# A step's whole turns counted ahead of the scans of the step before it, and one planned cost raised

## The reference

```python
x = x + 0.5 * ffn(layernorm(x))     # 8 experts, top 2 of them, and a shared one
x = x + attn(layernorm(x))
x = x + 0.5 * ffn(layernorm(x))
# attn, K = 32 heads, H = 8, M = 8 angles
phi = k_val[..., None] * theta                  # b, l, K, H, M
re_k, im_k = cos(phi), sin(phi)
cs = cumsum(concat([p_w, p_w * re_k, p_w * im_k]), axis=1)
state_re, state_im = num_re / den, num_im / den
out_re = sum(state_re * q_re + state_im * q_im, axis=-1)
out_im = sum(state_im * q_re - state_re * q_im, axis=-1)
# a gated projection of out_re and out_im, and W_out
```

## Time and profile before

| | |
|---|---|
| median of 3 runs | 1212.84 us (1212.49 to 1217.21) |
| profiled execution, its own time | 1213.98 us |
| span of the profile | 1212.6 us |
| PE, DVE, ACT, POOL busy | 1038.2, 729.8, 647.4, 483.2 us |
| TensorE clock granted, mean | 0.94 |

### The profile page before, as it was taken

How to read it: one execution, slowest core, us unless ns; L and a number is a source line. 1 busy time by engine, 2 the same in 40 slices (tenths; PEclk the granted TensorE clock), 3 DMA queues, 4 the chain that set the end, 5 groups by cost and what they waited for, 6 DMA issues and landing times.

```text
span 1212.6 us, 11351 instructions
## 1 busy us (share of the span) xinstructions
PE 1038.2 (86%) x3424; PEld 570.9 (47%) x3424; DVE 729.8 (60%) x1210; ACT 647.4 (53%) x1104; POOL 483.2 (40%) x451
## 2 busy tenths in 40 slices
PE   5887999868899889899879979985987899979993
PEld 3454544534445554334545434442554644436661
DVE  2320017698899899689969978994996931200000
ACT  4343334488546685445775675344588851414441
POOL 3454522353525542431632414521483431155542
PEclk9988999989999989899879989987999999989997
DMA  9876662666735866653856754353785763225666
GB/s 315 303 238 157 117 147 61 166 156 114 156 112 135 216 159 124 166 140 92 234 123 132 180 121 128 100 147 79 161 192 119 153 112 63 69 79 99 114 109 104
DMA packets 68978, 172.54 MB, mean 142 GB/s; under 512 B 12355, under 2 KB 12355, under 8 KB 66791
## 3 DMA queue, kind: packets, MB, share of 16 engines
q0 software_dynamic: 32576, 72.44, 33.2%
q1 hardware_dynamic: 36342, 99.38, 26.6%
HBM read 112.86 MB, written 68.33 MB: 149 GB/s over the span
## 4 chain that ended last, share of the span: by engine, by line
PE 31%; ACT 7%; DMA 5%; issue 3%; DVE 3%; POOL 1%; SPq 1%; DVEq 0%; ACTq 0%; POOLq 0%
PE hps L854 7%; PE yps L870 6%; PE misc L932 5%; PE yps L812 5%; PE hps L800 4%; DMA outT<-tail_sb 2%; DMA out_rows<-ys,into_i 1%; DMA x_rows<-ys,rows_i 1%; ACT L1036 1%; ACT ys L1049 1%; ACT hidden_sb L1036 1%; PE misc L923 1%; SPq L1855 1%; PE xps L923 1%; PE xps L845 1%
## 5 line engine op out<-in xcount | busy, mean ns | idle before, releaser
L870 PE MATMUL yps<-w_all,hidden_sb 128*128 x424 | 213.9, 629 | 39.7 <-ACT hidden_sb L1036 39.5
L854 PE MATMUL hps<-w_all,hidden_sb 128*128 x848 | 219.0, 404 | 25.3 <-ACT hidden_sb L1036 16.4
L1641 POOL DMA_INDIRECT xs<-x_normal,rows_i x106 | 124.1, 1171 | 216.2 <-PE xps L845 164.7
L854 PEld LDWEIGHTS hps<-w_all,hidden_sb 128*128 128x128 f32 x848 | 166.1, 202 | 80.7 <-issue 60.8
L1441 DVE TENSOR_TENSOR_SCAN run<-pwx,trig 128x512 f32<-128x512 f32 x128 | 149.3, 1207 | 24.8 <-ACT trig L1124 24.4
L1665 POOL DMA_INDIRECT x_rows<-ys,rows_i x56 | 101.6, 1813 | 105.5 <-ACT ys L1049 99.1
L870 PEld LDWEIGHTS yps<-w_all,hidden_sb 128*128 128x128 f32 x424 | 81.3, 200 | 117.8 <-issue 115.1
L1049 ACT ACTIVATE ys<-yps,slots 128x512 f32<-128x512 f32 x106 | 73.0, 689 | 110.9 <-PE yps L870 90.4
L800 PE MATMUL hps<-xnT,sw_sb 128*128 128x512 f32 x256 | 120.9, 621 | 6.5 <-ACT hidden_sb L1009 6.5
L812 PE MATMUL yps<-sw_sb,hidden_sb 128*128 128x512 f32 x256 | 120.8, 615 | 0.0
L1627 POOL DMA_INDIRECT slots<-told,dest_i x64 | 75.3, 1176 | 54.0 <-DVE cmp_a L1310 30.3
(11 more groups left out here) (202 smaller groups left out, 1531.1 us busy)
## 6 DMA issues: line engine op xcount, KB each, us to landing
qx<-q_cols SPq DMA_DIRECT2D x128, 256.0 KB
w_all<-in_w_experts SPq DMA_DIRECT2D x8, 1024.0 KB, 10.3
x_normal<-xin SPq DMA_DIRECT2D x32, 256.0 KB, 4.6
xin<-x_rows SPq DMA_DIRECT2D x32, 256.0 KB, 6.7
turns_sb<-in_w_out SPq DMA_DIRECT2D x3, 1536.0 KB, 13.7
xin<-in_x SPq DMA_DIRECT2D x16, 256.0 KB, 5.3
sum_rows<-ys SPq DMA_DIRECT2D x16, 256.0 KB, 3.0
xin<-sum_rows POOLq DMA_DIRECT2D x16, 256.0 KB, 8.2
```

Of the source, the lines that this page charges most:

```text
L854: t = PE.matmul(hps[:, bank, 0:H], xT[:, j % 2, c, :], w_all[:, bass.ds(expert[j] + c * H, H)], start=c == 0, stop=c == KC - 1)
L870: t = PE.matmul(yps[:, bank, :], hb[:, j % 2, ec, :], w_all[:, bass.ds(expert[j] + (KC * H + ec * D), D)], start=ec == 0, stop=ec == EC - 1)
L1641: GE.indirect_dma_start(xs[:, j % NX, :], None, xn_rows[PAIR_OF[g]], bass.IndirectOffsetOnAxis(rows_i[:, g % 2, j:j + 1], 0)).then_inc(*xs ...
```

## The change

Two edits. One raises the planned cost of the DVE stage `("load", 7)` from 1.2 to 11; the stage's instructions stay as they are. The other splits `phases`: the whole-turns instruction, with the waits that it had, becomes `whole_turns`, stage `c_int`. The DVE list is gone through after the planning: where a `c_scan` is directly followed by a `c_turn`, that turn's `c_int` is put in front of the scan; where a `c_turn` follows anything else, its `c_int` stands directly in front of it, as before.

```diff
-            piece("DVE", ("load", q), 1.2 if q == NJ - 1 else 3.4, ("SP", ("fetch", q), 3.6),
+            piece("DVE", ("load", q), 11 if q == NJ - 1 else 3.4, ("SP", ("fetch", q), 3.6),
...
         ORDERS = orders()
+        VECTOR = []
+        for i, s in enumerate(ORDERS["DVE"]):
+            then = ORDERS["DVE"][i + 1] if i + 1 < len(ORDERS["DVE"]) else ("end",)
+            if s[0] == "c_scan" and then[0] == "c_turn":
+                VECTOR.append(("c_int", *then[1:]))
+            if s[0] == "c_turn" and ORDERS["DVE"][i - 1][0] != "c_scan":
+                VECTOR.append(("c_int", *s[1:]))
+            VECTOR.append(s)
...
-            def phases(b, n):
+            def whole_turns(b, n):
                 half, m = divmod(n, M)
-                s = n % 2
-                th = theta_sb[:, half, m:m + 1]
                 if b > 0 or n >= 2:
                     last = (b, n - 2) if n >= 2 else (b - 1, STEPS + n - 2)
                     vec.wait_ge(*(out_summed if last[1] % M else added).at((*last, 0)))
                 vec.wait_ge(*convolved.at((b, half, CW - 1)))
-                VE.tensor_scalar(trig_int[:, s, 0, :], kept(b, half), th, None, ALU.mult).then_inc(*phase_int.of((b, n)))
+                VE.tensor_scalar(trig_int[:, n % 2, 0, :], kept(b, half), theta_sb[:, half, m:m + 1], None,
+                                 ALU.mult).then_inc(*phase_int.of((b, n)))
+
+            def phases(b, n):
+                half, m = divmod(n, M)
+                s = n % 2
                 vec.wait_ge(*phase_int.at((b, n)))
-                VE.scalar_tensor_tensor(trig[:, s, 1, :], kept(b, half), th, trig_int[:, s, 0, :],
+                VE.scalar_tensor_tensor(trig[:, s, 1, :], kept(b, half), theta_sb[:, half, m:m + 1], trig_int[:, s, 0, :],
                                         ALU.mult, ALU.subtract).then_inc(*phase_made.of((b, n)))
...
-            for stage, *at in ORDERS["DVE"]:
+            for stage, *at in VECTOR:
...
+                elif stage == "c_int":
+                    whole_turns(*at)
```

## The result

The change makes the kernel slower: 1221.3 us in the median of 20 runs, against 1214.6 us in the median of 20 runs of the kernel before on the same chip. The ratio is 1.0074, 95% interval 1.0048 to 1.0101. The forecast was 1206.5 us, in a range of 1198 to 1220: wrong in sign, and outside its range. The profiled execution of the changed kernel took 1226.88 us, for a span of 1225.5. That is 5.6 us above the median of its own runs, so the two profiles stand 12.9 us apart where the medians stand 6.7.

A forecast was written before the change was run, and what follows sets the result against it. No single engine was taken to bound the kernel: PE and DVE were about equally busy from 205 to 970 us. 3.8 + 2.6 = 6.4 us off 1212.84 gave 1206.4, stated as 1206.5, range 1198 to 1220.

The forecast's parts named there:

- the first term: Attention steps on DVE: counting ahead of the scans at 37 steps saves 7.6 us of DVE time, half booked, 3.8.
- The step that failed: DVE, whole turns to fraction: the dependence costs 0.11 us a step, covered by scans at 37 steps, 4.1 us.
- The second half of that term: DVE scans waiting for ACT's sine: the 0.39 us count fits into nine of these waits, 3.5 us.
- The second term: New planned order, ACT and PE near 700 us: gate before exponential closes PE holes, 2.6 us, bounds 0 and 4.3.
- the turns: PE, last nine blocks of group 4: three groups of small matmuls come earlier in the order, costed at nothing.
- rival C: Near 828 us: new order moves the output clear of the weight load, PE's 10.3 us hole closes; about 1199, chance 0.15.
- A: Whole kernel: both terms gain as forecast, own range 1201 to 1210.5 us, chance 0.40.
- the place at 700 us: ACT's gate goes ahead of the gates' exponential, letting gate matmuls fill PE's 4.81 us hole; 2.6 us taken.
- D: Near 828 us: output scaling or weight load planned later, PE's wait grows; 1213.5 to 1217, or 1224; chance 0.20.
- B: Attention middle: the DVE time saved is given back in PE's waits for moved outputs; 1212 us, chance 0.25.
- The chance for slower by over 0.5%: Whole kernel over 1218.9 us: PE's moved-output wait grows by more than 12.4 us, or unseen collisions; chance 0.15.

The follow-up runs named there:

- experiment 1: The changed kernel with the planner's old cost, so only the count ahead of the scans; 1223.2 us, 1.0079 of the kernel before.
- experiment 3: Count ahead in the old order, with the fraction also waiting for the scans ahead of it; 1210.2 us, 0.9953 of the kernel before.
- experiment 2: The kernel before with only the new planned cost, so the new order alone; 1207.5 us, 0.9948 of the kernel before.
- experiment 7: The kernel before, planned with one ACT gate ahead of the gates' exponential; 1209.6 us, 0.9957 of the kernel before.
- experiment 12: The kernel before, order kept, with a fraction that doesn't read the count and waits for nothing; 1249.6 us, 1.0292 of the kernel before.
- 5: The changed kernel with the fraction also waiting for the scans ahead of it; 1207.5 us, 0.9937 of the kernel before.
- 10: VectorE steps on constant tiles beside independent GpSimd work, without the kernel's computation; gathers 3.24 us each without a wait, 1.45 with one.

## Why the prediction was wrong

The forecast was made of two terms, 3.8 us for the earlier count and 2.6 for the new order.

**The step that failed** is in the first term: "the dependence costs 0.11 us a step", so "37 x 0.11 = 4.1 us of DVE time go". The 0.11 us are real and they did go. But they were booked as pure loss, with a lower bound of 0 for taking them out. They hold the rest ahead of the fraction, and it keeps POOL from being held up. Without it POOL instructions stand up to 6.8 us, and now and then one of them is what everybody waits for. Measured, the term is +0.8% (experiment 1), about 9.5 us slower, in place of 3.8 us faster. The missed sign could have been looked for: the prediction asks who waits behind DVE, and never who works beside it.

**The second half of that term had the right direction, and was too small.** "Nine of these, 15.5 us, lie at a place where the count comes ahead", 3.5 us. With the rest put back the count ahead gains 0.47% (experiment 3), 5.7 us at 1213.7, where half of 3.5 was booked, and the scans' wait falls by 8.9 us, not by 3 to 4. The prediction capped the gain at each wait by the count's own length, 0.39 us. Some waits shrink by more: the scan at 918.02 in the earlier trace rows waited 5.25 us, and 1.61 in experiment 3. That the sine comes earlier because the fraction does is the likely reason, not one that was followed through.

**The second term** had the right mechanism at its place, except that no table load was spared, and was undersized: 2.6 us taken, bounds 0 and 4.3, measured 6.3 (0.52% of 1213.7, experiment 2; the interval runs from 2.8 to 9.8, so the bound of 4.3 isn't refuted). The gate alone gives 0.9957, so the turns need have no part in it (experiment 7). PE's waits for the moved output are 3.2 us in kernel 2, which looks like rival C in company with A; but kernel 7 gains about as much with 8.8 us of them, so that what lies beyond the place at 700 us stays open.

**The rivals.** D, slower by a collision of output and weight load, isn't what happened: PE's waits for the moved output are 8.5 us in the changed kernel, the longest 3.4, less than the 11.7 and 10.3 of the earlier trace rows. That the measured 1221.3 lies between two of D's times, 1217 and 1224, is luck. B holds for neither part. The chance for slower by over 0.5%, 0.15, stood in part on "what collisions I don't see would add", and it was one of those.

**The cost of the semaphore, and the shared ports.** The rule of the Trainium skill in "VectorE: DVE Perf Modes", section "The DRAIN you can't avoid", was weighed: the semaphore costs nothing extra. The traces disagree by 0.11 us of DVE's own time, before and after. The page of the Trainium skill that was needed is "SBUF — State Buffer", section "Who interferes with whom": VectorE and GpSimd share a pair of ports, it is an exclusive lock, and a DMA issued by GpSimd suffers, since its descriptors are made there. This case agrees with the direction (a gather 0.96 us alone, 1.1 to 1.5 on average beside one kind of DVE instruction or steps with a wait). The same section of the Trainium skill also names the form: a VectorE instruction with two SBUF inputs contends with what GpSimd reads. By that section the lock, of which it says so for the two-port modes, is held for one whole instruction. That doesn't contain the size: the longest instruction of a step is 1.22 us, and here POOL stands 6 us over eight of them. Read as written it would have given a price of at most that 1.22 us for each POOL instruction, before and after alike, and no term for the edit.

**What stays open.** That a DVE without a rest before the fraction slows POOL, and that this is the loss, is shown: by taking the rest away with nothing moved (12), by putting it back (3, 5), and by the two engines alone (10). Why a POOL instruction that begins beside the fraction is held for so long and let through in the scans, why the fraction's per-partition operand matters, and why a rest after the sums helps in one setting and not in the other, is not; no theory here covers all three. Nor is it shown what each of the 20 long instructions costs: the two places above can be followed, while the 28.9 us that POOL was busier from 205 to 680 cost no time by 672.

## What to carry to other kernels

When a wait is to be taken from an engine, ask not only who stands behind that engine but who works beside it: here a rest of VectorE that shows as 0.04 us of idle time a step kept GpSimd's instructions short, and doing without one cost some 13 us (experiment 1 against 3) where 4 of VectorE's time at most were to be had. After such an edit compare the mean duration of every untouched group, GpSimd's first; the same work at a longer duration points to contention. The view of waits and the chain that ended last show only that GpSimd is waited for (ScalarE 24.7 us for its `rstd_ffn` before and 31.5 after; 1% of the chain before and 5% after), and nothing of VectorE's part in it. Where a reordering is good but takes away a rest, put the rest back by a wait on something nearly done, at the place where it stood, and measure the parts of a change one by one, since a gain of 0.5% hid inside a loss of 0.7%.

## What the runs showed of the hardware

- A GpSimd instruction can be held up over many VectorE instructions: 6.8 us for an indirect DMA (1.8 on average before), 8.3 in experiment 12, 6.1 us for a product of 128 by 4 (1.04 to 1.53 for the other eleven in the changed kernel), and 25.0 us for one gather beside count and fraction in turn.
- One wait for each 8 us of VectorE work, with 0.04 us (before) or 0.11 us (experiment 3) of idle time behind it, removes nearly all of it when it stands ahead of the fraction (1 long instruction against 13), and hardly any between sums and count (12). In the loops a constant in place of the fraction's per-partition operand removed it too (gathers of 1.46 us on average against 3.26, one stretch of eight steps each).
- VectorE's busy time doesn't show the conflict: it falls (727.3 us, and 723.8 in experiment 12, against 729.8) while GpSimd's grows by 52 and 94 us.
- Where a VectorE instruction waits for the one in front of it, it starts 0.04 us after the shown end of a count and 0.11 us after that of the scans (experiment 3); without the wait it starts 0.08 us before that end.
